# The TensorE program of sequences three to seven of the second attention: loop or straight code

## What is computed

```python
q, k = rope(hs @ Wq.T), rope(hs @ Wk.T); v = hs @ Wv.T
s = clip(hs @ Ws1.T @ Ws2.T + bs2, -32, 32)          # 64 slots
es, enz = exp(s), exp(-cumlogsumexp(s))
A  = where(mask, q k^T * scale, 0)
ok = enz * (A @ es);  qv = softmax(ok)
W2 = where(mask, (qv * enz) @ es^T, 0);  o = W2 @ v
out = (rmsnorm(o) * g_norm * silu(hs @ Wg.T)) @ Wo.T
```

## Time and profile before

| what | us |
|---|---|
| median of 3 executions | 1880.08 |
| lowest and highest | 1878.42, 1880.09 |
| the profiled execution, whole | 1896.83 |
| its span, from the first to the last instruction | 1895.0 |
| PE busy in the span | 1768.4 (93%) |
| DVE, ACT, POOL busy | 1265.7, 908.8, 857.2 |
| share of PE in the chain that ended last | 78% |
| mean granted TensorE clock | 0.975 |

### The profile page before, as it was taken

One profiled execution on the slowest core, in us unless ns is written; L12 is line 12 of the kernel. 1 busy time (PEld: TensorE's weight loads), 2 busy tenths in 40 slices (PEclk: granted clock), 3 DMA queues, 4 the chain that ended last, 5 costly groups with the idle time before them and its releaser, 6 DMA issues.

```text
span 1895.0 us, 34165 instructions
## 1 busy us (share of the span) xinstructions
PE 1768.4 (93%) x11310; PEld 1401.9 (74%) x11310; DVE 1265.7 (67%) x2787; ACT 908.8 (48%) x2986; POOL 857.2 (45%) x943
## 2 busy tenths in 40 slices
PE   6999988899879999999999999999999997999976
PEld 4666666677658887888888888888888885777653
DVE  4888988643676888886767666666666663444465
ACT  3777767543334444444544544445445443444321
POOL 2011024100665655657767667677676661000264
PEclk8999999999989999999999999999999998999998
DMA  7965543244220000000000000000001223333333
GB/s 238 304 217 164 187 140 112 92 129 142 99 85 1 1 12 1 6 1 15 21 16 15 20 16 20 16 12 23 13 12 45 85 102 123 107 106 107 100 118 108
DMA packets 104692, 148.39 MB, mean 78 GB/s; under 512 B 11888, under 2 KB 84720, under 8 KB 102096
## 3 DMA queue, kind: packets, MB, share of 16 engines
q1 hardware_dynamic: 95168, 119.95, 19.6%
q0 software_dynamic: 9216, 25.18, 4.0%
q10 hardware_dynamic: 144, 1.05, 0.1%
HBM read 81.64 MB, written 64.49 MB: 77 GB/s over the span
## 4 chain that ended last, share of the span: by engine, by line
PE 78%; DVE 10%; issue 4%; POOL 3%; ACT 2%; another core or an unknown queue 1%; DMA 1%; SPq 0%; DVEq 0%; ACTq 0%; POOLq 0%
PE ps L1419 12%; PE ps L1434 9%; PE ps L1506 5%; PE ps L1952 5%; PE ps L1460 5%; PE ps L705 4%; PE ps L1448 3%; PE ps L1447 3%; PE ps L1446 3%; PE ps L959 2%; PE ps L1441 2%; PE ps L1969 2%; PE ps L1971 2%; PE ps L724 2%; PE ps L695 2%
## 5 line engine op out<-in xcount | busy, mean ns | idle before, releaser
L1419 PE MATMUL ps<-work,weights 128*128 128x256 f32 x1024 | 248.6, 386 | 1.2 <-DVE work L1692 1.1
L1434 PE MATMUL ps<-split 128*128 128x512 f32 x768 | 227.8, 419 | 0.0
L1419 PEld LDWEIGHTS ps<-work,weights 128*128 128x128 f32 x1024 | 186.3, 191 | 23.8 <-DVE work L1692 1.4
L1834 POOL TENSOR_TENSOR work<-work,rope 128x512 f32<-128x512 f32 x128 | 164.8, 1288 | 54.0 <-ACT work L1607 54.0
L2147 POOL DMA_INDIRECT work<-yg,work x64 | 62.7, 980 | 238.7 <-DMA yg<-work 207.3
L1840 POOL TENSOR_TENSOR work<-work 128x512 f32<-128x512 f32 x128 | 164.5, 1285 | 5.0
L1434 PEld LDWEIGHTS ps<-split 128*128 128x128 f32 x768 | 130.7, 190 | 24.8
L827 DVE COPY work<-ps 128x384 f32<-128x384 f32 x256 | 130.0, 549 | 19.8 <-PE ps L705 19.5
L810 ACT ACTIVATE work<-ps,work 128x128 f32<-128x128 f32 x256 | 94.5, 369 | 84.5 <-DVE work L907 74.5
L705 PE MATMUL ps<-ident,work 128*128 128x128 f32 x768 | 115.4, 282 | 17.3 <-DVE work L827 15.4
L1506 PE MATMUL ps<-weights,work 128*128 128x256 f32 x512 | 124.1, 386 | 2.5 <-ACT work L1663 2.5
(11 more groups left out here) (240 smaller groups left out, 4447.3 us busy)
## 6 DMA issues: line engine op xcount, KB each, us to landing
heads_by_part<-split SPq DMA_DIRECT2D x64, 256.0 KB, 4.1
split<-heads_by_part SPq DMA_DIRECT2D x64, 256.0 KB
work<-xg SPq DMA_DIRECT2D x118, 128.0 KB
yg<-work SPq DMA_DIRECT2D x118, 128.0 KB, 1.7
xg<-work SPq DMA_DIRECT2D x13, 1024.0 KB, 5.9
weights<-in_w SPq DMA_DIRECT2D x8, 1024.0 KB, 6.1
weights<-in_f SPq DMA_DIRECT2D x8, 1024.0 KB, 5.0
weights<-in_f SPq DMA_DIRECT2D x8, 608.0 KB, 4.4
```

The lines of the kernel that those rows point to most:

```text
L1419: last = pe.matmul(ps[:, 2, which * SEQ:(which + 1) * SEQ], w1(h, (which * KC + kc) * P, P), xT[:, kc, :], start=kc == 0, stop=kc == KC - 1)
L1434: last = pe.matmul(ps[:, 3, :], x1_split[:, xp, kc, c * P:(c + 1) * P], w_vg[:, n % 2, wp, kc, :], start=i == 0, stop=i == KC * len(TERMS) ...
L1834: pool.tensor_tensor(qk[:, h % 4, :, :], raw[:, h % 2, :, :], rope[:, 0, :].unsqueeze(1).broadcast_to([P, 2, SEQ]), ALU.mult).then_inc(rot ...
```

## The change

On TensorE alone, the hardware loop over t = 2 to 6 becomes a Python loop, which writes the five bodies one behind the other. The instructions of the body, their order and the waits are the same; t is a constant in each copy, so that wait values are constants. The programs of the other engines stay as they are, VectorE's and ScalarE's loops included.

```diff
             pe_slots(pe, 0, "first")
             pe_slots(pe, 0, "middle")
             pe_slots(pe, 1, "middle", True)
-            with pe.Fori(2, SEQ_END) as t:
+            for t in range(2, SEQ_END):
                 pe_slots(pe, t, "middle")
             pe_slots(pe, SEQ_END, "last")
             pe_blocks1(pe)
```

## The result

The changed kernel takes 1861.76 us (median of 4, 1860.02 to 1864.71) against 1880.09 for the kernel before in the same sets: ratio 0.9906, 95% interval 0.9891 to 0.9922, so 18.3 us less. The prediction said 1862.8. Two later sets on other occasions gave 0.9906 and 0.9915 again.

What follows compares the result with a forecast made beforehand. TensorE was taken to bound the kernel, idling at four taken loop branches; 10.9 us of gap plus 6.4 us of half clock made 17.3 us, and 1880.08 - 17.3 = 1862.8 us, range 1859 to 1866.

Steps and rivals of the forecast that it cites:

- What bounds: Second attention: TensorE, busy 93% of the span, sets the time, so its idle moments there are kernel time.
- rival 2: Sequence boundaries: other engines become the bound, 2.3 us each, leaving a gain of 8.1 us, 1872.0 us; chance 0.05.
- The gap, 10.9 us: Turns after sequences 2 to 5: removing four taken TensorE branches removes their idle gaps, 10.88 us together.
- The half clock, 6.4 us: First pair behind each of four turns: half-clock stretches go with the gaps, 16.5 us becoming 14.90, 6.40 us together.
- its lower bound: Half-clock term at the turns: gain could be 0, since without the profiler the clock may not fall.
- Rival 1: Turns: the gap goes but the clock's part is not there to gain, 10.9 us, 1869.2 us; chance 0.13.
- The sum, 17.3 us: Four turns: gap 10.9 plus half clock 6.4 us, subtracted from the 1880.08 us median to give 1862.8.
- In the loop they are fetched again on each turn anyway.: TensorE's looped body: code is refetched each turn, so straight code lowers fetches by about 3 a turn.
- a rival: Sequence ends: body fits the 2048-instruction buffer, so the stall isn't the branch and straight code keeps it, 1880; chance 0.02.
- Code is costed at 0.: TensorE's four added bodies: fetches come ahead of use, 0 us; at most 2.9 us at each boundary.
- some ten fetches fewer: Queue 8 in the changed kernel's profile: some ten code fetches fewer than in five sequences before.

Runs made afterwards that it cites:

- the hint: Looped kernel of before plus one instruction at the head of TensorE's body naming its closing branch, so the target can be fetched ahead: 1864.70 us, ratio 0.9920.
- slot 208: Looped kernel of before, no hint, with padding that puts the head of TensorE's body on slot 208 of a 256-instruction block: 1881.38 us, ratio 1.0017.
- covered loop: Looped kernel of before with six more matmuls, their result unread, at the end of each looped body, queued ahead of the branch: 1879.74 us, ratio 0.9999.
- slot 100: Looped kernel of before, no hint, with padding that puts the head of TensorE's body on slot 100 of a 256-instruction block: 1863.68 us, ratio 0.9921.
- slot 0: Looped kernel of before, no hint, with the head of TensorE's body put on the first slot of a block: 1863.02 us, ratio 0.9911.

## Why the prediction was right

- **What bounds.** Right: PE carried the chain at the boundaries, and every microsecond taken from its gap came off the time. VectorE was not late (rival 2 fell): the first pairs behind the four boundaries are as long as any other, 14.9 us.
- **The gap, 10.9 us.** Right, and its cause shown: the hint alone removes it.
- **The half clock, 6.4 us.** Right in size: first pairs of 14.9 for 16.5 at all four. The bare loop at slot 208 loses 17.3 us in the stretch, the sum predicted, though split otherwise: 11.8 on the pairs with the gap and 5.5 on the first pairs, since its clock fell at three turns of four. That the two deviations cancel is luck. So the term can be smaller in an execution, as its lower bound allowed. In the covered loop the clock's part disappears with a short gap, which shows that it hung on the gap; that not every long gap brings it, slot 208 shows. Rival 1 (10.9 us alone, 1869.2) is not what the medians show.
- **The sum, 17.3 us, put on the median.** Measured 18.3, 17.7 and 16.0 in three sets. The stretch of the profiled execution of before was 19.2 us longer, 1.9 more than its turns. 0.5 us of it are the four pairs with the gap, longer by 11.35 us than straight ones where the gaps are 10.88. The rest lies in ordinary pairs, of which one or two a sequence took 15.06 to 15.10 us for 14.90 and one 16.71 for 16.53; slot 208, with the same four turns, has none of them. What they were stays open; the medians don't show that the change removes them.
- **"In the loop they are fetched again on each turn anyway."** This step was true of this kernel, and wrong as I meant it, as a property of loops with a long body. The same body is kept, and its branch costs 0.2 us, if its head lies 100 slots into a block or at its start. I had the right rule in hand, the 2048 instructions of the Trainium skill, and set it aside as a rival because this trace spoke against it. Both were true: the body fits in the buffer and did not lie so that it was kept. So the time was forecast rightly for this kernel, by a step that would have failed for the same loop with its head elsewhere in its block.
- **"Code is costed at 0."** Right: the straight kernel's 25 blocks between the boundaries arrive without a gap at any pair, and it is as fast as the loops that fetch none. The forecast of some ten fetches fewer came true, 96 for 107.

## What to carry to other kernels

A gap before the first instruction of a loop body that ends in "issue" is worth a look at the sequencer's own branch record: 0.2 us is a branch, 3 to 4 us is a branch that waits for its code. Writing the loop out, a hint at the body's head, or another place for the head in its block give the same stretch here and medians within 3 us, so the choice can go by code size. Telling whether a body is kept needs no other kernel: a kept one has no row for its instruction queue while it turns. The converse is a warning for any change: instructions added or removed ahead of a long loop shift its head, and that alone may move a kernel such as this by 18 us, 1%, which would be put down to the edit itself. By the estimate above the kernel before stood only a few instructions over that edge; no run moved it by so few.

## What the runs showed of the hardware that I had not expected

- One looped body of 1636 instructions, once fetched, was run four times more with no code fetched for some 480 us (slot 100, slot 0, or with the hint), and fetched afresh on each turn at slot 208. Six blocks fetched in its first pass went with the one, seven with the other.
- TensorE's compare-and-branch by kind, from these runs: falls through 76 to 83 ns, taken back with the target's code there 207 to 259 ns, taken back with the code to be fetched 3337 to 3899 ns. The jump forward over the padding took 191 to 333 ns.
- The clock fell to 1.2 GHz behind gaps of 2.57 to 3.13 us in which PE had nothing queued, at eight of the nine gaps of that size that the bare loops of three kernels left; at the ninth, of 3.12 us, it stayed. It did not fall behind the eight gaps of 0.39 to 0.90 us. Where it falls it costs 1.5 to 1.6 us, on top of the gap.
